# Attention scores: the mask and the row maximum enter the scores through a turned operand, high and low part in one contraction

## The chip, the cores and the metric

The kernel runs on one core of one Trainium2 chip. The metric is the device time of the whole program in microseconds; lower is better. Three timed runs of the kernel before gave 849.24, 849.87 and 851.15 us, median 849.87 us. The trace is of one further, profiled execution.

## The reference

A gated cross-attention layer and a mixture of experts, both with a residual. There are 128 sequences of 64 tokens, width 128, 16 heads of 8 channels, and a context of 64 tokens for each sequence. What matters here is the attention:

```
q, k, v = heads(layernorm(x) @ Wq.T + bq), heads(ctx @ Wk.T + bk), heads(ctx @ Wv.T + bv)
scores  = q k^T / sqrt(8)
scores  = where(pad_mask[key] == 0, -1e9, scores) + src_mask[query, key]
x       = x + tanh(g_xattn) * (softmax(scores) v @ Wo.T + bo)
```

Then `x + tanh(g_ffn) * ffn(layernorm(x))` follows, where ffn takes the two best of 8 experts for each token, a shared expert, and a layer norm. The padding mask depends on the sequence and the key, the source mask on the query and the key.

## The kernel before, in words

Three stages follow one another: `attention` (to about 450 us), `experts` and `combine`. Only the first is touched.

In `attention` a tile is 128 tokens, that is two sequences, b = 0 and 1, on the partitions (64 queries each). There are 64 tiles, and four of them make a quad. Each engine has its own program, written out by hand: a step n handles one tile, and u = n mod 4 is its place in the quad. Work that belongs to a quad (projections of the next quad, its layer norm, its mask, the routing of an earlier one) is put at fixed places u of the steps. Engines meet by semaphores (`need` waits for one). Every engine works strictly in its own order.

TensorE's step n is, in this order: the prefix sums of the routing (u = 1), `project_out(n - 3)`, `scores(n)`, `feed_a` (transposes or a projection for the quad, none at u = 0), `values(n - 2)`, `turn(n - 1)` (eight transposes of the probabilities, L394), `feed_b` (more of the quad's work, L450, L456, L462 or L469), `subtract(n)`.

- `scores` writes 128 x 1024 scores (16 heads of 64 keys) into two PSUM banks in 64x64 tiles of the array (L366). Then it adds the mask with four matmuls of 512 columns (L372): an identity is multiplied with the mask of the queries, spread over 8 heads, once with the high part and once with the low part of the mask, for either half of the heads. The parts are there because the matmuls read the type fp32r, which holds fewer bits than float32.
- `maxima` on VectorE (L531) takes the negated maximum of every query and head. `max_high` and `max_low` (L536, L540) split it into two parts.
- `subtract` (L383) adds the maxima in the same manner: four matmuls of 512 columns, identity times the high or low part, spread over the 64 keys.
- ScalarE takes the exponential from PSUM (L856), the transposes go to PSUM and ScalarE copies them back (L895), `values` forms the sums and the products with v (L403, L410), VectorE divides (L546, L551), and `project_out` multiplies with Wo (L418).

VectorE's step has eight numbered places between its parts. The mask of the next quad is made at u = 2 in four steps (L710, L714, L717, L719), at places 2, 4, 5 and 7; place 2 is before `maxima`, place 4 between `max_high` and `max_low`, place 5 before the reciprocal, place 7 at the end. At u = 3, place 1 adds a bias to a quad of x (L726) and place 2 runs eight aggregations (L585, L586), both before `maxima`. Maxima of tile n need `masked` (the last of the mask's matmuls).

SyncE loads for each quad the context, the padding mask spread to queries by two transfers (`pad_q`, L318) and the padding mask spread to all partitions (`pad_k`, L319).

ScalarE's step has the exponential of tile n - 1 first, then the quad's copies, then the two copies of the turned probabilities.

Of the kernel before, what the change touches and what calls it, by code (L numbers as in the profile page):

```python
# [26 lines left out]
P = 128  # L27
# [28 lines left out]
C_SEL = C_PART + 1  # L56
C_TOKEN = C_SEL + 2

# [26 lines left out]
def constants(NT):  # L85
    c = np.zeros((P, C_TOKEN + NT + steps_listed(NT)), np.float32)
    p = np.arange(P)
    c[:, C_ID:C_ID + P] = np.eye(P)
    c[:, C_TRI:C_TRI + P] = p[:, None] < p[None, :]
    c[:, C_JM:C_JM + HG] = (p[:, None] % 32) // DK == np.arange(HG)[None, :]  # L90
    c[:, C_REV:C_REV + QT * E] = np.tile(E - np.arange(E), QT)
    c[:, C_BASE:C_BASE + E] = np.arange(E) * (NT * P + SL)
    c[:, C_PART] = p
    c[:, C_SEL:C_SEL + 2] = ((p[:, None] // 32) % 2 == np.arange(2)[None, :]) * float(DK) ** -0.5
    c[:, C_TOKEN:C_TOKEN + NT] = NT * P + p[:, None] + P * np.arange(NT)[None, :]
    c[:, C_TOKEN + NT:] = np.arange(steps_listed(NT))
    return c
# [73 lines left out]
def attention(nc, a, NT, lists, m):  # L171
# [6 lines left out]
    with ExitStack() as ctx:  # L178
# [5 lines left out]
        ones_bf = sb("ones_bf", [P, P], BF16)  # L184
        ident_r = sb("ident_r", [P, P])
        w_att = sb("w_att", [P, 4, D])
# [7 lines left out]
        rb = router[:, 32:33]  # L194
        srcm = sb("srcm", [P, S])
        cT = sb("cT", [P, 2, QW])
        pad_q = sb("pad_q", [P, 2, QT, S], I32)
        pad_k = sb("pad_k", [P, 2, QW], I32)
        keep = sb("keep", [P, QW])
        mask = sb("mask", [P, QT, S])  # L200
        mask_hl = sb("mask_hl", [P, 2, 2, QT, S])
        xn = sb("xn", [P, QW])
# [7 lines left out]
        mx = sb("mx", [P, 2, H])  # L210
        mx_hl = sb("mx_hl", [P, 2, 2, H])
        head_ones = sb("head_ones", [P, VS])
# [44 lines left out]
        keep_ready, mask_step, mask_ready, xb_ready = sem("keep_ready"), sem("mask_step"), sem("mask_ready"), sem("xb_ready")  # L257
        masked, maxed, max_split, subbed, exped = (sem(n) for n in ("masked", "maxed", "max_split", "subbed", "exped"))
        turned, PT_ready, att_done, recips, aT_ready = (sem(n) for n in ("turned", "PT_ready", "att_done", "recips", "aT_ready"))
        wo_done, x2_ready = sem("wo_done"), sem("x2_ready")  # L260
# [14 lines left out]
        def exists(item, total):  # L275
            return 0 <= item < total

        LOADS = 4
        CONSTS = 16 * 7
        MASK_STEPS = 4  # L280

# [4 lines left out]

        def wide_mask(part, par, u):

            return mask_hl[:, part, par, u, :].bitcast(F32R).unsqueeze(1).broadcast_to([P, H // 2, S])

# [4 lines left out]
        def _(sp):  # L295
            sp.dma_start(cst[:, :], a["consts"]).then_inc(const_in, 16)
            for t, n in ((w_att, "w_att"), (srcm, "src_mask"), (router, "router"), (cols[:, 0:3], "b_att")):
                sp.dma_start(t if n == "b_att" else t[:], a[n]).then_inc(const_in, 16)
# [9 lines left out]
            def load(q, par):  # L308

                need(sp, v_done, q - 2, total=NQ)  # L310
                need(sp, mask_step, q - 2, per=MASK_STEPS, total=NQ)
                need(sp, kT_ready, q - 2, total=NQ)
                done = quad_in[par]
                sp.dma_start(cT[:, par, :], a["ctx_T"][:, bass.ds(q * QW, QW)]).then_inc(done, 16)
                pads = pad_mask[bass.ds(q * 2 * QT, 2 * QT), :]
                for b in range(2):
                    src = pads.rearrange("(t b) k -> b t k", b=2)[b:b + 1].broadcast_to([S, QT, S])
                    sp.dma_start(pad_q[b * S:(b + 1) * S, par], src).then_inc(done, 16)  # L318
                sp.dma_start(pad_k[:, par].rearrange("p (b k) -> p b k", k=S),  # L319
                             pads.unsqueeze(0).broadcast_to([P, 2 * QT, S])).then_inc(done, 16)  # L320
# [25 lines left out]
        def _(pe):  # L346
# [7 lines left out]
            def scores(n, u, par, q):  # L354
# [118 lines left out]
            def step(j):  # L473
                for v in range(2 * QT):
# [29 lines left out]
        def _(ve):  # L504
# [20 lines left out]
            ve.reciprocal(gates[:, 2:3], gates[:, 2:3]).then_inc(setup_dve, 1)  # L525
            ve.tensor_copy(ident_r[:, :].bitcast(F32R), ident).then_inc(setup_dve, 1)

# [6 lines left out]
            def max_high(n, u):  # L534
                need(ve, maxed, n)
                ve.tensor_copy(mx_hl[:, 0, u % 2, :].bitcast(F32R), mx[:, u % 2, :]).then_inc(max_split, 1)  # L536

            def max_low(n, u):
                need(ve, max_split, n, per=2, k=1)
                ve.tensor_tensor(mx_hl[:, 1, u % 2, :].bitcast(F32R), mx[:, u % 2, :], mx_hl[:, 0, u % 2, :],  # L540
                                 ALU.subtract).then_inc(max_split, 1)

# [161 lines left out]
            def masks(i, j, par, q):  # L704

                p2 = 1 - par
                if i == 0:
                    quad_loaded(ve, j, par, 1)
                    need(ve, mask_step, q, per=MASK_STEPS, total=NQ)
                    ins = ve.tensor_scalar(mask[:, :, :], pad_q[:, p2], 0, NEG, ALU.is_equal, ALU.mult)  # L710
                else:
                    need(ve, mask_step, q + 1, per=MASK_STEPS, k=i, total=NQ)
                if i == 1:
                    ins = ve.tensor_tensor(mask[:, :, :], mask[:, :, :], srcm[:, :].unsqueeze(1).broadcast_to([P, QT, S]),  # L714
                                           ALU.add)
                elif i == 2:
                    ins = ve.tensor_copy(mask_hl[:, 0, p2].bitcast(F32R), mask[:, :, :])  # L717
                elif i == 3:
                    ins = ve.tensor_tensor(mask_hl[:, 1, p2].bitcast(F32R), mask[:, :, :], mask_hl[:, 0, p2],  # L719
                                           ALU.subtract)  # L720
                ins.then_inc(mask_step, 1)
# [28 lines left out]
            def between(place, j, u, par, q):  # L750
# [22 lines left out]
                elif u == 2:  # L773
                    if exists(q + 3, NQ):
# [4 lines left out]
                        elif place == 7:  # L779
                            in_stats(j, par, q, 3, (3,))  # L780
                    if place in (2, 4, 5, 7) and exists(q + 1, NQ):
                        masks((2, 4, 5, 7).index(place), j, par, q)
                else:
# [41 lines left out]
        def _(ac):  # L825
# [22 lines left out]
            def step(j):  # L848
                for v in range(2 * QT):
# [646 lines left out]
def build_inputs(inputs):  # L1496
# [4 lines left out]
    f32["mask_BxS2_ik0"] = g["mask_BxS2_ik0"]  # L1501
    f32["src_mask"] = np.concatenate([g["mask_1x1xSxS2_ff0"][0, 0]] * 2)
    f32["w_att"] = np.stack([g["L0_xattn_" + n].T for n in ("Wq", "Wk", "Wv", "Wo")], axis=1)
# [33 lines left out]
```

## Time and profile before

| what | value |
|---|---|
| timed runs | 849.24, 849.87, 851.15 us |
| profiled execution, its time | 852.03 us |
| its span, first to last instruction | 850.0 us |
| mean granted TensorE clock | 0.941 |
| PE busy | 726.5 us, 85% |
| PE weight loads busy | 591.4 us, 70% |
| VectorE busy | 612.2 us, 72% |
| ScalarE busy | 508.1 us, 60% |
| GpSimd busy | 285.0 us, 34% |

PE is TensorE's matmuls and PEld its weight loads, which may run beside matmuls. Busy times are those of instruction records. Matmuls overlap in the array, so the sum of their durations is more than the time they take one after another. The granted clock is a share of full speed, and 1.00 and 0.50 are TensorE's two levels of 2.4 and 1.2 GHz.

### The profile page before, as it was taken

What the parts mean: (1) busy time and instruction counts of PE and PEld (TensorE: products, weight loads), DVE (VectorE), ACT (ScalarE), POOL (GpSimd) and SP (SyncE); (2) the same over time, 40 slices, a digit from 0 to 9 for tenths busy, and PEclk for the clock granted to TensorE, in tenths of its full rate; (3) what the DMA queues carried; (4) which work ended last, traced back from release to release, by engine and by line L of the source; (5) the groups of instructions that cost most, each with busy time, mean ns of one, the idle gap of its engine ahead of it and who ended that gap; (6) DMA issues with size and microseconds to landing.
All of it is one profiled execution on the core that took longest, in us unless ns stands there. A gap on an engine that the chain in (4) does not pass through costs nothing. (4 is left out here: it accounts for less than half of the span.)

```text
span 850.0 us, 25318 instructions
## 1 busy us (share of the span) xinstructions
PE 726.5 (85%) x8266; PEld 591.4 (70%) x8267; DVE 612.2 (72%) x2341; ACT 508.1 (60%) x1051; POOL 285.0 (34%) x293
## 2 busy tenths in 40 slices
PE   2899999999999999999961029999999999969870
PEld 1577777777777777777740019899999999956650
DVE  5477778778887888877772648766666666627998
ACT  2667777777677776767431006566666666628983
POOL 2000022233332233322257404565555555630000
PEclk9999999999999999999985559999999999989995
DMA  5122212233312233210011662222222222234553
GB/s 128 44 46 46 57 48 59 65 80 82 80 49 62 61 83 83 74 46 33 22 61 63 207 121 58 72 75 75 75 75 77 75 75 72 78 108 128 152 150 96
DMA packets 84289, 66.60 MB, mean 78 GB/s; under 512 B 17008, under 2 KB 71536, under 8 KB 84208
## 3 DMA queue, kind: packets, MB, share of 16 engines
q1 hardware_dynamic: 63008, 35.49, 17.5%
q0 software_dynamic: 8448, 17.45, 6.2%
q10 hardware_dynamic: 12752, 12.58, 4.6%
q8 instruction: 51, 0.84, 0.4%
q14 instruction: 30, 0.25, 0.1%
HBM read 38.21 MB, written 23.09 MB: 72 GB/s over the span
## 5 line engine op out<-in xcount | busy, mean ns | idle before, releaser
L167 POOL DMA_INDIRECT expert_lists<-xn,slots x128 | 128.5, 1004 | 337.8 <-PE pair L410 305.8
L1129 ACT ACTIVATE hT<-pair,b1g_c,gate_c 128x256 f32<-128x256 f32 x272 | 138.3, 562 | 93.6 <-PE pair L76 83.0
L1276 POOL DMA_INDIRECT expert_results<-y,dest x136 | 144.5, 1062 | 130.0 <-DVE y L1245 109.0
L1089 PE MATMUL pair<-w,hT 128*128 x1088 | 134.5, 277 | 0.1
L1089 PEld LDWEIGHTS pair<-w,hT 128*128 128x128 f32 x1088 | 127.0, 192 | 2.7 <-issue 2.0
L531 DVE TENSOR_REDUCE mx<-pair 128x16 f32<-128x1024 f32 x64 | 78.4, 1225 | 46.6 <-PE pair L372 46.6
L856 ACT ACTIVATE prob<-pair 128x1024 f32<-128x1024 f32 x64 | 65.5, 1024 | 45.8 <-PE pair L383 45.7
L895 ACT ACTIVATE PT<-pair 128x512 f32<-128x512 f32 x128 | 69.3, 593 | 38.5 <-PE pair L394 38.5
L74 PE MATMUL pair<-rT,w_now 128*128 128x256 f32 x276 | 84.5, 306 | 2.4 <-DVE rT L68 2.4
L76 PE MATMUL pair<-rT,w_now 128*128 128x256 f32 x276 | 78.9, 286 | 0.0
L75 PE MATMUL pair<-rT,w_now 128*128 128x256 f32 x276 | 78.6, 285 | 0.0
L1216 DVE CAST w_now<-w 128x1024 fp32r x71 | 50.4, 711 | 38.2 <-issue 37.0
L383 PE MATMUL pair<-mx_hl,ident_r 128*128 128x512 f32 x256 | 75.8, 419 | 1.3 <-DVE mx_hl L540 1.3
L372 PE MATMUL pair<-mask_hl,ident_r 128*128 128x512 f32 x256 | 76.9, 422 | 0.0
L366 PE MATMUL pair<-kbd,qg 64*64 64x256 f32 x1024 | 71.0, 393 | 0.0
L394 PE MATMUL pair<-cst,prob 128*128 128x128 f32 x512 | 69.9, 280 | 0.0
L1067 PE MATMUL pair<-cst,rows 128*128 128x128 f32 x140 | 27.3, 277 | 44.3 <-DMA rows<-expert_lists 44.3
L372 PEld LDWEIGHTS pair<-mask_hl,ident_r 128*128 128x128 f32 x256 | 43.4, 189 | 30.6 <-issue 25.0
L546 DVE RECIPROCAL rsum<-pair 128x128 f32<-128x128 f32 x64 | 60.7, 948 | 0.7 <-PE pair L410 0.7
L394 PEld LDWEIGHTS pair<-cst,prob 128*128 128x128 f32 x512 | 54.9, 141 | 5.8
L74 PEld LDWEIGHTS pair<-rT,w_now 128*128 128x128 f32 x276 | 53.4, 193 | 4.1 <-issue 3.7
L66 DVE CAST rT<-pair 128x256 fp32r<-128x256 f32 x70 | 29.6, 424 | 36.4 <-PE pair L1067 36.3
(171 smaller groups left out, 1438.3 us busy)
## 6 DMA issues: line engine op xcount, KB each, us to landing
rows<-expert_lists SPq DMA_DIRECT2D x70, 130.0 KB, 2.2
yin<-expert_results SPq DMA_DIRECT2D x16, 512.0 KB, 5.3
x_all<-in_x SPq DMA_DIRECT2D x16, 256.0 KB, 5.0
cT<-in_ctx_T SPq DMA_DIRECT2D x16, 256.0 KB, 2.9
pad_k<-in_mask_BxS_ik SPq DMA_DIRECT2D x16, 256.0 KB, 4.9
xn2T<-x2T ACTq DMA_DIRECT2D x16, 256.0 KB, 2.4
out<-res ACTq DMA_DIRECT2D x7, 512.0 KB, 4.7
expert_results<-y,dest POOLq DMA_INDIRECT x136
```

The source lines that it names most:

```text
L74: pe.matmul(out, ah, bh, start=True, stop=False)
L75: pe.matmul(out, ah, bl, start=False, stop=False)
L76: return pe.matmul(out, al, bh, start=False, stop=True)
L167: po.indirect_dma_start(lists[:, :], bass.IndirectOffsetOnAxis(ap=m.slots[:, par, t, k:k + 1], axis=0), m.xn2[:, par, t, :], None).then_in ...
L366: pe.matmul(ps[S * b:S * b + S, at:at + 256], qg[rows, par, s, u * P + S * b:u * P + S * b + S], kbd[rows, par, 2 * u + b].rearrange("p j ...
L372: i = pe.matmul(ps[:, half * 512:(half + 1) * 512].rearrange("p (h k) -> p h k", k=S), ident_r[:, :].bitcast(F32R), wide_mask(part, par, u ...
L383: i = pe.matmul(ps[:, half * 512:(half + 1) * 512].rearrange("p (h k) -> p h k", k=S), ident_r[:, :].bitcast(F32R), top.unsqueeze(2).broad ...
L394: t = pe.transpose(pt_ps[h][:, i * P:(i + 1) * P], prob[:, u % 2, p * P:(p + 1) * P], ident)
L531: ve.tensor_reduce(mx[:, u % 2, :], sc_ps[u % 2][:, :].rearrange("p (h k) -> p h k", k=S), X, ALU.max, negate=True).then_inc(maxed, 1)
L1089: last = pe.matmul(y_ps[par][:, h * D:(h + 1) * D], hT[:, par, c, h * P:(h + 1) * P], w2[:, bass.ds(e, 1), c, :].rearrange("p a d -> p (a ...
L1129: ac.activation(hT[:, par, c, :], h_ps[par][c // 2][:, (c % 2) * SL:(c % 2 + 1) * SL], ACT.Gelu, bias=b1g_c[:, c, bass.ds(e, 1)], scale=ga ...
L1276: po.indirect_dma_start(results[:, :], bass.IndirectOffsetOnAxis(ap=dest[:, par, h, :], axis=0), y[:, par, h, :], None).then_inc(sent[par] ...
```

## The change

The roles of the operands in the mask's and the maximum's matmuls are exchanged.

- Mask: the mask is now kept with the key on the partition and the query in the free dimension. The high part stands on partitions 0 to 63 and the low part on 64 to 127. It is the stationary operand, and a constant selector of keys (`key_r`, 1 where the partition modulo 64 is the key) is the moving one, so a contraction over 128 partitions adds both parts. Two matmuls instead of four for a tile.
- Maximum: `max_high` and `max_low` write the parts into a 128 x 128 tile, two copies at columns 0 to 31 and 64 to 95. TensorE turns 96 columns of it with one transpose (`turn_maxima`, into the scores buffer of the other tile), ScalarE copies that to `mT`, and `subtract` contracts 32 rows (16 heads, high and low) with a constant selector of heads (`head_r`). The first half of the heads uses rows 0 to 31, the second rows 64 to 95. Two matmuls instead of four for a tile.
- The mask of a quad is made from a constant source mask, turned on the host, and padding columns that are computed once, so `pad_q` and its two transfers for each quad are gone, and there is one more constant to load. The mask's steps are three instead of four, and place 4 is empty.

```diff
-                    for part in range(2):
-                        i = pe.matmul(ps[:, half * 512:(half + 1) * 512].rearrange("p (h k) -> p h k", k=S),
-                                      ident_r[:, :].bitcast(F32R), wide_mask(part, par, u),
-                                      start=False, stop=False, skip_group_check=True)
+                    i = pe.matmul(ps[:, half * 512:(half + 1) * 512].rearrange("p (h k) -> p h k", k=S),
+                                  mask_hl[:, par, 2 * u:2 * u + 2, :].rearrange("p b q -> p (b q)").bitcast(F32R),
+                                  key_r[:, :].bitcast(F32R).unsqueeze(1).broadcast_to([P, H // 2, S]),
+                                  start=False, stop=False, skip_group_check=True)
                 i.then_inc(masked, 1)
 
+            def turn_maxima(n, u):
+                need(pe, max_split, n, per=2)
+                need(pe, exped, n - 1)
+                pe.transpose(sc_ps[(u + 1) % 2][0:S + 2 * H, 0:P], mx_hl[:, u % 2, 0:S + 2 * H], ident)\
+                  .then_inc(max_turned, 1)
+
             def subtract(n, u):
-                need(pe, max_split, n, per=2)
+                need(pe, max_flat, n)
                 ps = sc_ps[u % 2]
                 for half in range(2):
-                    for part in range(2):
-                        top = mx_hl[:, part, u % 2, half * 8:half * 8 + 8].bitcast(F32R)
-                        i = pe.matmul(ps[:, half * 512:(half + 1) * 512].rearrange("p (h k) -> p h k", k=S),
-                                      ident_r[:, :].bitcast(F32R), top.unsqueeze(2).broadcast_to([P, H // 2, S]),
-                                      start=False, stop=(part == 1), skip_group_check=True)
+                    rows = slice(S * half, S * half + 2 * H)
+                    i = pe.matmul(ps[:, half * 512:(half + 1) * 512].rearrange("p (h k) -> p h k", k=S),
+                                  mT[rows, u % 2, :].bitcast(F32R),
+                                  head_r[rows, half * 8:half * 8 + 8].bitcast(F32R).unsqueeze(2)
+                                  .broadcast_to([2 * H, H // 2, S]),
+                                  start=False, stop=True, skip_group_check=True)
                 i.then_inc(subbed, 1)
...
                         values(n - 2, (u - 2) % QT, par if u >= 2 else 1 - par)
+                    if exists(n, NT):
+                        turn_maxima(n, u)
                     if exists(n - 1, NT):
                         turn(n - 1, (u - 1) % QT)
...
             ve.tensor_copy(key_r[:, :].bitcast(F32R), cst[:, C_KEY:C_KEY + S]).then_inc(setup_dve, 1)
+            ve.tensor_copy(head_r[:, :].bitcast(F32R), cst[:, C_HEAD:C_HEAD + H]).then_inc(setup_dve, 1)
+            ve.tensor_scalar(pad_neg[:, :], pad_T[:, :], 0, NEG, ALU.is_equal, ALU.mult).then_inc(setup_dve, 1)
+            ve.memset(mx_hl[:, :, :], 0.0).then_inc(setup_dve, 1)
+            ve.wait_ge(setup_dve, 15)
...
-                ve.tensor_copy(mx_hl[:, 0, u % 2, :].bitcast(F32R), mx[:, u % 2, :]).then_inc(max_split, 1)
+                ve.tensor_copy(both_copies(mx_hl, u, 0).bitcast(F32R), mx[:, u % 2, :].unsqueeze(1).broadcast_to([P, 2, H]))\
+                  .then_inc(max_split, 1)
...
-                    ins = ve.tensor_scalar(mask[:, :, :], pad_q[:, p2], 0, NEG, ALU.is_equal, ALU.mult)
+                    pads = pad_neg[:, (q + 1) * 2 * QT:(q + 2) * 2 * QT]
+                    ins = ve.tensor_tensor(mask[:, :, :], srcT[:, :].unsqueeze(1).broadcast_to([P, 2 * QT, S]),
+                                           pads.unsqueeze(2).broadcast_to([P, 2 * QT, S]), ALU.add)
...
                 if i == 1:
+                    ins = ve.tensor_copy(mask_hl[:, p2].bitcast(F32R), mask[:, :, :])
                 elif i == 2:
+                    ins = ve.tensor_tensor(mask_hl[S:, p2].bitcast(F32R), mask[S:, :, :], mask_hl[S:, p2], ALU.subtract)
...
+                    if exists(n, NT):
+                        need(ac, max_turned, n)
+                        need(ac, subbed, n - 2)
+                        ac.activation(mT[0:S + 2 * H, u % 2, :].bitcast(F32R), sc_ps[(u + 1) % 2][0:S + 2 * H, 0:P],
+                                      ACT.Copy).then_inc(max_flat, 1)
```

The last piece stands in ScalarE's step just before the copies of the turned probabilities of tile n - 1.

## Rows read from the trace of the kernel before

**Rows 1.** Busy time in a stretch: us, busy us (count) by engine, clock, DMA share, GB/s.
```profile
200.00:300.00 100.00, 100.00 (x1415) 74.27 (x1414) 80.32 (x334) 71.71 (x134) 32.01 (x32) 1.00 0.27 70
```

**Rows 2.** Waits, 60 to 370 us: waiter, releaser, us in total, times, longest.
```profile
DVE mx L531 <- PE pair L372: 26.2, 48, 0.8
```

**Rows 3.** Timeline of PE, 204 to 230 us: start, us, line, op, count [idle before].
```profile
203.77 0.40 PE L372 MATMUL pair<-mask_hl,ident_r 128*128 128x512 f32 x1
...
205.12 1.09 PE L394 MATMUL pair<-cst,prob 128*128 128x128 f32 x8
...
209.49 1.20 PE L372 MATMUL pair<-mask_hl,ident_r 128*128 128x512 f32 x4
...
212.08 1.09 PE L394 MATMUL pair<-cst,prob 128*128 128x128 f32 x8
...
214.31 0.39 PE L418 MATMUL pair<-w_att,aT 128*128 128x128 f32 x2
214.62 1.09 PE L366 MATMUL pair<-kbd,qg 64*64 64x256 f32 x16
215.65 1.21 PE L372 MATMUL pair<-mask_hl,ident_r 128*128 128x512 f32 x4
...
218.66 1.09 PE L394 MATMUL pair<-cst,prob 128*128 128x128 f32 x8
219.68 0.43 PE L462 MATMUL pair<-x2T,router 128*32 128x128 f32 x8
...
222.34 1.19 PE L372 MATMUL pair<-mask_hl,ident_r 128*128 128x512 f32 x4
...
224.60 1.09 PE L394 MATMUL pair<-cst,prob 128*128 128x128 f32 x8
...
228.63 1.20 PE L372 MATMUL pair<-mask_hl,ident_r 128*128 128x512 f32 x4
```

**Rows 4.** Timeline of VectorE, one tile at u = 0: from maximum to low part.
```profile
204.21 1.23 DVE L531 TENSOR_REDUCE mx<-pair 128x16 f32<-128x1024 f32 x1 [0.58 <-PE pair L372]
...
205.68 0.18 DVE L540 TENSOR_TENSOR mx_hl<-mx,mx_hl 128x16 fp32r<-128x16 f32 x1
```

**Rows 5.** L383 at tile 0, and L372 at 202 us: duration ns min/median/max, starts.
```profile
L383 PE MATMUL pair<-mx_hl,ident_r x4: 379/379/484, 31.5 to 32.3; 128*128 128x512 f32 x4
```
```profile
L372 PE MATMUL pair<-mask_hl,ident_r x4: 393/398/496, 203.0 to 203.8; 128*128 128x512 f32 x4
```

**Rows 6.** Timeline of PE weight loads around tile 0's subtraction.
```profile
31.51 0.73 PEld L383 LDWEIGHTS pair<-mx_hl,ident_r 128*128 128x128 f32 x4 [1.70 <-DVE mx_hl L540]
```

**Rows 7.** Timeline of VectorE: the maxima of the tiles at u = 2 and 3.
```profile
216.89 1.23 DVE L531 TENSOR_REDUCE mx<-pair 128x16 f32<-128x1024 f32 x1 [0.83 <-PE pair L372]
...
223.58 1.22 DVE L531 TENSOR_REDUCE mx<-pair 128x16 f32<-128x1024 f32 x1 [0.32 <-PE pair L372]
```

**Rows 8.** Groups by line, 60 to 370 us: shapes, count, busy us, mean ns, idle before.
```profile
L726 DVE TENSOR_TENSOR x_all<-x_all,bo_row 128x512 f32<-128x512 f32 x12 | 8.1, 674 | 0.0
...
L714 DVE TENSOR_TENSOR mask<-mask,srcm 128x256 f32<-128x256 f32 x12 | 5.0, 419 | 0.0
L719 DVE TENSOR_TENSOR mask_hl<-mask,mask_hl 128x256 fp32r<-128x256 f32 x12 | 4.9, 407 | 0.0
...
L903 ACT ACTIVATE LT<-pair,router 128x128 f32<-128x128 f32 x11 | 4.1, 371 | 0.0
...
L717 DVE CAST mask_hl<-mask 128x256 fp32r<-128x256 f32 x12 | 3.5, 295 | 0.0
L710 DVE TENSOR_SCALAR mask<-pad_q 128x256 f32<-128x256 int32 x12 | 3.3, 276 | 0.0
```

**Rows 9.** Timeline of ScalarE at u = 1, ahead of the copies of probabilities.
```profile
212.05 0.71 ACT L845 ACTIVATE kbd<-kT,cst 128x512 f32<-128x512 f32 x1
```

**Rows 10.** Timeline of the start: a constant's transfer is issued, VectorE's setup.
```profile
3.52 0.43 SPq L300 DMA_DIRECT2D gates<-in_gates  x1
```
```profile
9.13 0.21 DVE L526 CAST ident_r<-cst 128x128 fp32r<-128x128 f32 x1
```

More of the change, by code:

```diff
@@ L56 @@
 C_SEL = C_PART + 1
-C_TOKEN = C_SEL + 2
+C_KEY = C_SEL + 2
+C_HEAD = C_KEY + S
+C_TOKEN = C_HEAD + H
 def split(ve, done, high, low, x):
@@ L94, in constants @@
     c[:, C_SEL:C_SEL + 2] = ((p[:, None] // 32) % 2 == np.arange(2)[None, :]) * float(DK) ** -0.5
+    c[:, C_KEY:C_KEY + S] = p[:, None] % S == np.arange(S)[None, :]
+    c[:, C_HEAD:C_HEAD + H] = (p[:, None] % S < 2 * H) & (p[:, None] % H == np.arange(H)[None, :])
     c[:, C_TOKEN:C_TOKEN + NT] = NT * P + p[:, None] + P * np.arange(NT)[None, :]
@@ L184, in attention @@
         ones_bf = sb("ones_bf", [P, P], BF16)
-        ident_r = sb("ident_r", [P, P])
+        key_r = sb("key_r", [P, S])
+        head_r = sb("head_r", [P, H])
         w_att = sb("w_att", [P, 4, D])
@@ L194, in attention @@
         rb = router[:, 32:33]
-        srcm = sb("srcm", [P, S])
+        srcT = sb("srcT", [P, S])
+        pad_T = sb("pad_T", [P, 2 * NT], I32)
+        pad_neg = sb("pad_neg", [P, 2 * NT])
         cT = sb("cT", [P, 2, QW])
-        pad_q = sb("pad_q", [P, 2, QT, S], I32)
         pad_k = sb("pad_k", [P, 2, QW], I32)
         keep = sb("keep", [P, QW])
-        mask = sb("mask", [P, QT, S])
-        mask_hl = sb("mask_hl", [P, 2, 2, QT, S])
+        mask = sb("mask", [P, 2 * QT, S])
+        mask_hl = sb("mask_hl", [P, 2, 2 * QT, S])
         xn = sb("xn", [P, QW])
@@ L210, in attention @@
         mx = sb("mx", [P, 2, H])
-        mx_hl = sb("mx_hl", [P, 2, 2, H])
+        mx_hl = sb("mx_hl", [P, 2, P])
+        mT = sb("mT", [P, 2, P])
         head_ones = sb("head_ones", [P, VS])
@@ L258, in attention @@
         masked, maxed, max_split, subbed, exped = (sem(n) for n in ("masked", "maxed", "max_split", "subbed", "exped"))
+        max_turned, max_flat = sem("max_turned"), sem("max_flat")
         turned, PT_ready, att_done, recips, aT_ready = (sem(n) for n in ("turned", "PT_ready", "att_done", "recips", "aT_ready"))
@@ L276, in exists @@
             return 0 <= item < total
-        LOADS = 4
-        CONSTS = 16 * 7
-        MASK_STEPS = 4
+        LOADS = 2
+        CONSTS = 16 * 8
+        MASK_STEPS = 3
         J0, J1 = -1, NQ // 2 + 2
@@ L285, in cols_of, with both_copies @@
             return bass.ds(t * D, n * D)
-        def wide_mask(part, par, u):
-            return mask_hl[:, part, par, u, :].bitcast(F32R).unsqueeze(1).broadcast_to([P, H // 2, S])
+        def both_copies(t, u, part):
+            return t[:, u % 2, :].rearrange("p (c w) -> p c w", w=S)[:, :, part * H:part * H + H]
         block = ctx.enter_context(nc.Block())
@@ L296, in _ @@
             sp.dma_start(cst[:, :], a["consts"]).then_inc(const_in, 16)
-            for t, n in ((w_att, "w_att"), (srcm, "src_mask"), (router, "router"), (cols[:, 0:3], "b_att")):
+            for t, n in ((w_att, "w_att"), (srcT, "src_T"), (pad_T, "pad_T"), (router, "router"), (cols[:, 0:3], "b_att")):
                 sp.dma_start(t if n == "b_att" else t[:], a[n]).then_inc(const_in, 16)
@@ L315, in load @@
                 pads = pad_mask[bass.ds(q * 2 * QT, 2 * QT), :]
-                for b in range(2):
-                    src = pads.rearrange("(t b) k -> b t k", b=2)[b:b + 1].broadcast_to([S, QT, S])
-                    sp.dma_start(pad_q[b * S:(b + 1) * S, par], src).then_inc(done, 16)
                 sp.dma_start(pad_k[:, par].rearrange("p (b k) -> p b k", k=S),
@@ L525, in _ @@
             ve.reciprocal(gates[:, 2:3], gates[:, 2:3]).then_inc(setup_dve, 1)
-            ve.tensor_copy(ident_r[:, :].bitcast(F32R), ident).then_inc(setup_dve, 1)
+            ve.tensor_copy(key_r[:, :].bitcast(F32R), cst[:, C_KEY:C_KEY + S]).then_inc(setup_dve, 1)
+            ve.tensor_copy(head_r[:, :].bitcast(F32R), cst[:, C_HEAD:C_HEAD + H]).then_inc(setup_dve, 1)
+            ve.tensor_scalar(pad_neg[:, :], pad_T[:, :], 0, NEG, ALU.is_equal, ALU.mult).then_inc(setup_dve, 1)
+            ve.memset(mx_hl[:, :, :], 0.0).then_inc(setup_dve, 1)
+            ve.wait_ge(setup_dve, 15)
             def maxima(n, u):
@@ L535, in max_high @@
                 need(ve, maxed, n)
-                ve.tensor_copy(mx_hl[:, 0, u % 2, :].bitcast(F32R), mx[:, u % 2, :]).then_inc(max_split, 1)
+                ve.tensor_copy(both_copies(mx_hl, u, 0).bitcast(F32R), mx[:, u % 2, :].unsqueeze(1).broadcast_to([P, 2, H]))\
+                  .then_inc(max_split, 1)
             def max_low(n, u):
                 need(ve, max_split, n, per=2, k=1)
-                ve.tensor_tensor(mx_hl[:, 1, u % 2, :].bitcast(F32R), mx[:, u % 2, :], mx_hl[:, 0, u % 2, :],
-                                 ALU.subtract).then_inc(max_split, 1)
+                ve.tensor_tensor(both_copies(mx_hl, u, 1).bitcast(F32R), mx[:, u % 2, :].unsqueeze(1).broadcast_to([P, 2, H]),
+                                 both_copies(mx_hl, u, 0), ALU.subtract).then_inc(max_split, 1)
             def sums_inverse(n, u):
@@ L713, in masks @@
                 if i == 1:
-                    ins = ve.tensor_tensor(mask[:, :, :], mask[:, :, :], srcm[:, :].unsqueeze(1).broadcast_to([P, QT, S]),
-                                           ALU.add)
+                    ins = ve.tensor_copy(mask_hl[:, p2].bitcast(F32R), mask[:, :, :])
                 elif i == 2:
[L717 to L720, printed above, removed]
+                    ins = ve.tensor_tensor(mask_hl[S:, p2].bitcast(F32R), mask[S:, :, :], mask_hl[S:, p2], ALU.subtract)
                 ins.then_inc(mask_step, 1)
@@ L780, in between @@
                             in_stats(j, par, q, 3, (3,))
-                    if place in (2, 4, 5, 7) and exists(q + 1, NQ):
-                        masks((2, 4, 5, 7).index(place), j, par, q)
+                    if place in (2, 5, 7) and exists(q + 1, NQ):
+                        masks((2, 5, 7).index(place), j, par, q)
                 else:
@@ L1501, in build_inputs @@
     f32["mask_BxS2_ik0"] = g["mask_BxS2_ik0"]
-    f32["src_mask"] = np.concatenate([g["mask_1x1xSxS2_ff0"][0, 0]] * 2)
+    f32["src_T"] = np.concatenate([g["mask_1x1xSxS2_ff0"][0, 0].T] * 2)
+    f32["pad_T"] = np.concatenate([g["mask_BxS2_ik0"].T] * 2)
     f32["w_att"] = np.stack([g["L0_xattn_" + n].T for n in ("Wq", "Wk", "Wv", "Wo")], axis=1)
```

1 line of the change is left out of this document (removed).

## The prediction

> **What bounds the kernel now.** First I read the busy table by stretch, to find the limit of the stage that changes. In a stretch in its middle PE is busy for all 100.00 of 100 us at clock 1.00, against 80.32 us of VectorE and 71.71 us of ScalarE [rows 1]. The reader is to see an engine that never waits. The waits confirm it from the other side: VectorE waits for the mask's last matmul before each maximum, 26.2 us in 48 waits, so about 0.55 us of slack for each tile [rows 2]. So time is made by PE's own order, and I read its timeline tile by tile. A tile's last mask matmul ends at 203.77 + 0.40 = 204.17, the same point of the next quad is 228.63 + 1.20 = 229.83, so a quad lasts 25.66 us; the pattern repeats through the stage. I write every event relative to the end of a tile's mask matmuls, because that starts VectorE's chain. The transposes of the probabilities (L394) start at 0.95, 1.39, 1.80 and 1.07 us for u = 0, 1, 2, 3 [rows 3]. (The mask ends are 204.17, 210.69, 216.86 and 223.53.) The new transpose of the maxima stands just ahead of them, so these four numbers decide the case.
>
> **The mask's matmuls.** Four matmuls take 1.20 us. Without the last one's 0.40 and the first one's extra 0.10 (496 ns against 398, its weights being loaded in sight) they follow one another by (1.20 - 0.10 - 0.40)/3 = 0.23 us [rows 3, 5]. Two fewer save 0.46 us for each tile, 1.86 us for a quad. I take the two that remain at the same pace. A constant moving operand might run at the subtraction's pace of 0.217 (next part) but not slower in any row.
>
> **The subtraction.** Its four matmuls start from 31.5 to 32.3 and the first is 105 ns longer than the others when its weights are loaded after a wait [rows 5]. Weight loads there span 0.73 us for three intervals and a load of 0.19, or (0.73 - 0.11 - 0.19)/2 = 0.217 us for each matmul, one interval being short by the exposed first [rows 6]. The two new ones use different row groups (0 to 31, 64 to 95) and different banks. No row has this shape. Nearest are the scores: 16 records of 256 columns in 1.09 us, where two records of 128 columns in `project_out` start 0.39 - 0.28 = 0.11 apart (eight such in L394 take 1.09, which is seven paces of 0.11, 0.05 for the first load and a duration of about 0.27), so 256 columns alone take 0.22 and 16 in series would take 3.5 us [rows 3]. They run four at a time, two of them row halves into two banks. So the pair should start together, and one interval is left: saved 3 x 0.217 = 0.65 us a tile. The other end is a pair in series, saved 0.43 us. I take the first, by the scores.
>
> **New switches of the array's shape.** The array was in 128x128 shape from the transposes through `subtract` to `project_out`. Now `subtract` is in 32x128 shape. The price of a switch: `project_out`'s second matmul starts at 214.42, its pace would end it at 214.53, and the scores start at 214.62, so 0.09 us is lost; then the first matmul behind a bare 128-column load is 0.10 us longer [rows 3, 5]. That is 0.20 us on entry and 0.20 on exit. At u = 2 L462 has already left the shape, so the entry is free. Four exits and three entries make 1.4 us a quad; prefix sums behind the exit at u = 0 to 1 have cheap loads, so I take 1.32. Bounds: 0.09 for each switch if loads are hidden (0.63 a quad), and 0.20 for each of eight (1.6).
>
> The Trainium skill (TensorEngine Tiling, Key Properties) says "Changing tiling mode (not just tile) drains the TensorE". By that rule alone the seven switches cost the 0.09 that the trace shows as its drain, and the quad would gain 0.7 us more than in my sum; the rows put the exposed load beside it, so I keep 0.20. The trace agrees with the rule (the 0.09 us before the scores).
>
> **The new transpose.** One record of 128 columns at a pace of 0.11 us (1.09 - 0.27 over 7 intervals is 0.117, the first load's 0.05 among it) [rows 3]: +0.44 us a quad. Its load takes the exposed place that the first probability's load had.
>
> **The new wait, the heart of it.** Formerly the split maximum was needed by `subtract`, after the transposes and `feed_b`. Now it is needed before them. VectorE's chain from the mask's end: 0.04 to the reduction, and the low part ends at 205.68 + 0.18 = 205.86, that is 1.69 [rows 4]. Two splits write 32 instead of 16 values each (estimate +0.02 each, from 256 more values costing 0.27 us between L719 and L726 [rows 8]), and PE's load starts about 0.04 after the release: 1.77 us. At u = 2 a mask step stood between the splits and is gone, so 1.77 holds there too. Behind the waiting transpose stand the eight transposes of tile n - 1, `feed_b` and `subtract`, and all else of PE. Stalls without further delay: 0.82, 0.38, 0 and 0.70 us.
>
> Further delay comes because VectorE must be free when the mask ends, which is now 0.46 us earlier behind `project_out`. Its idle before the maximum was 0.58 at u = 0 and 0.83 at u = 2 and 0.32 at u = 3 [rows 4, 7]; I take 0.45 at u = 1 by the mean of rows 2. At u = 3 that is short by 0.14. At u = 2 the first mask step grows from 0.276 to 0.674 (L710 to the shape of L726), so 0.83 - 0.40 - 0.46 leaves -0.03 [rows 7, 8]. Stalls then: 0.82, 0.40, 0 and 0.85, sum 2.07 us.
>
> **VectorE's other work.** The mask was 0.276 + 0.419 + 0.295 + 0.407 = 1.40 us a quad; it becomes 0.674 (add), about 0.43 (cast of 512, by the slope of L717), 0.674 (64 partitions, 512 values): 1.78 [rows 8]. Together +0.38 and +0.16 for the splits, on an engine at 20.6 of 25.65. At 21.1 of 25.0 us it is still not the bound, so this costs nothing beyond the delays counted: the later mask steps lie behind the divide that `project_out` needs. If that cover went, 0.4 us a quad.
>
> **ScalarE's new copy** (96x128 from PSUM, by L903's 0.371 us [rows 8]) runs beside the eight transposes (0.88 us) and `feed_b` (0.4 to 0.9). At u = 1 ScalarE is busy until 212.05 + 0.71 = 212.76, or 2.07 after the mask's end [rows 9]; the turned maxima are there at about 1.8 + 0.33 = 2.1, so no delay arises. The copies of probabilities come 0.37 later and are used a step later. Cost nothing; if the cover went, 0.4 us a tile.
>
> **Loads.** `pad_q` goes, off the path. In the start one more constant is issued before the one that VectorE waits for (+0.47, an issue of 0.43 and its gap), and setup exchanges one cast of 0.21 for two casts, a scalar operation, a memset and a wait (smaller tiles than the cast's; estimate 0.15 each, less 0.2: +0.4) [rows 10]. VectorE's chain sets the start, so +0.9 us.
>
> **Sum.** A quad: stalls +2.07, mask -1.86, subtraction -2.60, transpose +0.44, switches +1.32: -0.63 us. Fourteen full quads: -8.8. The last quad has no `feed` work before the transposes, so all four tiles wait as at u = 0, 0.82 (3.3 together): +0.6. In the first, early tiles waited for VectorE already and the detour over ScalarE takes the place of the two saved matmuls: about +0.5. Start +0.9. Total -6.8 us: 852.03 - 6.8 = 845.2 for a profiled execution. That one lies 2.2 above the median of the runs, so the timed median should be 849.87 - 6.8 = **843.1 us**.
>
> **Rivals.**
> 1. *The pair of `subtract` runs in series* (slower). Place: L383's successors, 0.217 us more for each of 64 tiles, +13.9: 849.87 - 6.8 + 13.9 = 857.0. It decides as soon as more than half of the overlap is missing. For it: no row has 32x128 tiles, and two wide fp32r streams go at once. Against it: the scores' four at a time.
> 2. *The wait eats the gain.* The maximum's chain is later than 1.77 us, by 0.15 us at three tiles (VectorE not free, a slower split with two copies), or the switches cost 0.05 more each: +0.4 to 0.6 a quad, 849 to 850. For it: VectorE has only the slack above, and it grows. Against: stalls at u = 2 are nearly zero, which leaves that tile its full saving.
> 3. *Switches cost only their drain*, the loads being pulled ahead: -0.7 a quad more, 832 us. For it: weight loads run beside matmuls elsewhere. Against: the 105 and 100 ns in rows 5.
> 4. *The change doesn't do what it says*, the wide matmuls being no limit: excluded by the first reading, PE without idle.
>
> **Chances.** My forecast 0.60 (own range 838 to 848), rival 1 0.17, rival 2 0.14, rival 3 0.09. A change within 0.2% (1.7 us) is about what a measurement can't tell from none. Faster: 0.60 + 0.09 less a little = 0.68. Same: most of rival 2, 0.13. Slower: rival 1 and the rest, 0.19. The range 835 to 854 leaves out most of rival 1 and the end of rival 3. The forecast's number, 843.1.
>
> **What would show it.** Right: PE's timeline gets idle time or late loads before the new transpose, released by VectorE's low part, of about 0.8, 0.4, 0 and 0.85 us; the two L383 successors start within 0.01 us; gaps of 0.20 at both ends of them; the quad's period is 25.0. Wrong: the pair 0.217 apart; waits for ScalarE's copy in front of `subtract`; a period above 25.65.

## The result, and the profile after

Four timed runs of the changed kernel took 839.2 to 841.7 us, median 840.33, beside 850.47 for the kernel before. The ratio is 0.9873, with a 95% interval of 0.9856 to 0.9890: 1.3% faster. The forecast was 6.8 us less; 10.1 us by the medians and 10.8 by the ratio were measured, and the profiled span fell from 850.0 to 837.6. Here and below, executions more than 1.5% above the fastest of the same kernel are left out of medians and ratios (one of e1's ten, five of e5's ten, one of e7's six).

The first view is again the busy table by stretch. Its row answers rows 1.

```profile
200.00:300.00 100.00, 93.66 (x1444) 63.30 (x1445) 85.20 (x344) 78.09 (x155) 31.23 (x32) 1.00 0.23 67
```

PE is no longer busy all the time: it stands for 6.3 us of 100. The waits (rows 2 before) name the reason. VectorE's long wait for the mask's matmuls, 26.2 us before, is nearly gone (1.5 us). TensorE now waits for VectorE instead: 26 such waits stand in the some 50 tiles of that stretch, 17.7 us in all.

```profile
PE pair L385 <- DVE mx_hl L559: 17.7, 26, 1.1
...
PE pair L448 <- DVE kT L715: 2.2, 11, 0.2
DVE mx L549 <- PE pair L376: 1.5, 4, 0.4
```

PE's timeline of one quad answers rows 3 (L376 is the mask, L385 the new transpose, L406 the probabilities' transposes, L393 the subtraction):

```profile
199.67 0.73 PE L376 MATMUL pair<-key_r,mask_hl 128*128 128x512 f32 x2
...
202.16 0.31 PE L385 MATMUL pair<-cst,mx_hl 128*96 128x128 f32 x1 [0.74 <-DVE mx_hl L559]
202.31 1.04 PE L406 MATMUL pair<-cst,prob 128*128 128x128 f32 x8
...
206.26 0.73 PE L376 MATMUL pair<-key_r,mask_hl 128*128 128x512 f32 x2
207.20 0.63 PE L448 MATMUL pair<-cst,xn 128*128 128x128 f32 x4 [0.20 <-DVE kT L715]
...
208.81 0.31 PE L385 MATMUL pair<-cst,mx_hl 128*96 128x128 f32 x1
...
210.37 0.48 PE L393 MATMUL pair<-head_r,mT 32*128 32x512 f32 x2
210.78 0.49 PE L430 MATMUL pair<-w_att,aT 128*128 128x128 f32 x2
...
212.22 0.73 PE L376 MATMUL pair<-key_r,mask_hl 128*128 128x512 f32 x2
...
214.77 0.32 PE L385 MATMUL pair<-cst,mx_hl 128*96 128x128 f32 x1
...
218.10 0.74 PE L376 MATMUL pair<-key_r,mask_hl 128*128 128x512 f32 x2
...
220.61 0.31 PE L385 MATMUL pair<-cst,mx_hl 128*96 128x128 f32 x1 [0.65 <-DVE mx_hl L559]
...
224.47 0.73 PE L376 MATMUL pair<-key_r,mask_hl 128*128 128x512 f32 x2
```

A quad now takes 224.47 - 199.67 = 24.80 us, 0.86 less than [rows 3]. Counted from the end of each tile's mask matmuls, the new transpose starts at 1.76, 1.82, 1.82 and 1.77 us for u = 0 to 3, where L394 stood at 0.95, 1.39, 1.80 and 1.07. Two matmuls in 0.48 us, each of 478 ns, start together.

VectorE's timeline of the same tile (rows 4), the maximum at u = 3 (rows 7), and the setup (rows 10):

```profile
200.44 1.22 DVE L549 TENSOR_REDUCE mx<-pair 128x16 f32<-128x1024 f32 x1
...
201.92 0.19 DVE L559 TENSOR_TENSOR mx_hl<-mx,mx_hl 128x32 fp32r<-128x32 f32 x1
```
```profile
218.85 0.15 DVE L605 BATCH_NORM_AGGREGATE mv<-st 128x2 f32<-128x6 f32 x1
218.92 1.19 DVE L549 TENSOR_REDUCE mx<-pair 128x16 f32<-128x1024 f32 x1
```
```profile
7.20 0.23 DVE L520 CAST tri_bf<-cst 128x128 bf16<-128x128 f32 x1 [7.09 <-DMA gates<-in_gates]
```

The low part is ready 1.71 us after the mask's end (202.11 - 200.40). At u = 3 the maximum has no idle time before it any more: VectorE comes from its aggregations 0.05 us late.

### The profile page after: what moved, and what is told of

It is laid out like the page before. It is cut to its first block and busy times, and to the rows that moved or that the text cites. A ratio compares the mean times of both kernels' runs of the same rounds, so it can differ in the third digit from the quotient of the medians.

```text
span 837.6 us, 25065 instructions
## 1 busy us (share of the span) xinstructions
PE 686.2 (82%) x8074; PEld 537.2 (64%) x8075; DVE 621.1 (74%) x2328; ACT 523.3 (62%) x1115; POOL 280.5 (33%) x293
## 5 line engine op out<-in xcount | busy, mean ns | idle before, releaser
L171 POOL DMA_INDIRECT expert_lists<-xn,slots x128 | 124.3, 971 | 330.4 <-PE pair L422 297.9
L549 DVE TENSOR_REDUCE mx<-pair 128x16 f32<-128x1024 f32 x64 | 77.9, 1217 | 14.1 <-PE pair L376 12.6
L406 PE MATMUL pair<-cst,prob 128*128 128x128 f32 x512 | 66.4, 273 | 0.0
L576 DVE SCALAR_TENSOR_TENSOR x_all<-pair,gates,x_all 128x128 f32<-128x128 f32 x64 | 22.4, 351 | 53.6 <-PE pair L430 52.7
L406 PEld LDWEIGHTS pair<-cst,prob 128*128 128x128 f32 x512 | 56.6, 141 | 0.1
L76 PEld LDWEIGHTS pair<-rT,w_now 128*128 128x128 f32 x276 | 53.3, 193 | 3.3 <-issue 2.1
L77 PEld LDWEIGHTS pair<-rT,w_now 128*128 128x128 f32 x276 | 53.5, 194 | 0.0
L78 PEld LDWEIGHTS pair<-rT,w_now 128*128 128x128 f32 x276 | 53.3, 193 | 0.0
```

What stands on the lines that cost most here:

```text
L76: pe.matmul(out, ah, bh, start=True, stop=False)
L77: pe.matmul(out, ah, bl, start=False, stop=False)
L78: return pe.matmul(out, al, bh, start=False, stop=True)
L171: po.indirect_dma_start(lists[:, :], bass.IndirectOffsetOnAxis(ap=m.slots[:, par, t, k:k + 1], axis=0), m.xn2[:, par, t, :], None).then_in ...
L406: t = pe.transpose(pt_ps[h][:, i * P:(i + 1) * P], prob[:, u % 2, p * P:(p + 1) * P], ident)
L549: ve.tensor_reduce(mx[:, u % 2, :], sc_ps[u % 2][:, :].rearrange("p (h k) -> p h k", k=S), X, ALU.max, negate=True).then_inc(maxed, 1)
```

## The experiments

All ratios are to the kernel before on the same chip. Several chips were used. The code shown is one piece of each edit. On the chip of e1 to e4 the kernel before takes 852 us, about as for the result. Quads are means over tiles 16 to 51 of each trace.

| run | us | before | ratio, 95% interval | quad, us |
|---|---|---|---|---|
| changed kernel | 840.3 | 850.5 | 0.987 (0.986 to 0.989) | 24.81 |
| e1, pair in series | 855.2 | 852.2 | 1.005 (1.003 to 1.007) | 25.65 |
| e2, mask alone | 827.7 | 852.2 | 0.972 (0.969 to 0.975) | 24.25 |
| e3, maximum alone | 869.1 | 852.2 | 1.021 (1.017 to 1.024) | 26.80 |
| e4, transpose between | 826.1 | 852.2 | 0.970 (0.967 to 0.973) | 23.99 |
| e5, no switch | 893.0 | 892.3 | 1.000 (0.996 to 1.004) | 26.99 |
| e6, mask alone, keys early | 864.0 | 892.3 | 0.971 (0.966 to 0.975) | 24.68 |
| e7, between, keys early | 876.5 | 892.3 | 0.981 (0.978 to 0.985) | 25.02 |
| e8, behind, keys early | 869.4 | 892.3 | 0.974 (0.970 to 0.978) | 24.60 |
| e9, e8 again | 872.4 | 891.6 | 0.976 (0.970 to 0.982) | 24.59 |
| e10, e6 again | 863.0 | 891.6 | 0.965 (0.959 to 0.971) | 24.70 |
| e11, changed kernel again | 870.9 | 869.9 | 1.002 (1.000 to 1.004) | 26.30 |
| e12, e8 a third time | 845.8 | 869.9 | 0.973 (0.970 to 0.977) | 24.33 |

**e1: the pair of the subtraction in series**

```diff
-                    rows = slice(S * half, S * half + 2 * H)
+                    rows = slice(0, 2 * H)
```

> The changed kernel, with both matmuls of the subtraction on rows 0 to 31, so that they can't run side by side. Theory (the pair runs side by side and PE's order sets the time): the second one starts 0.217 us after the first, 64 x 0.217 = 13.9 us more than the changed kernel's 840.3, so 854. Rival (the two only start together, and the longer records and the late project_out show that the banks or the streams take turns): no more than 3 us more, 840 to 843.

```profile
203.13 0.69 PE L393 MATMUL pair<-head_r,mT 32*128 32x512 f32 x2
203.76 0.49 PE L430 MATMUL pair<-w_att,aT 128*128 128x128 f32 x2
```

The pair takes 0.69 instead of 0.48 us, the quad 0.84 us more (4 x 0.21), and the time is 855.2 for an expected 854. So the two row groups do run side by side, and the pair in series would have made the change a loss. The theory holds; rival 1 of the prediction falls.

**e2 and e3: each half by itself**

```diff
# e2: the changed kernel with the old subtraction
-                    if exists(n, NT):
-                        turn_maxima(n, u)
# e3: the kernel before with the new subtraction
+                    if exists(n, NT):
+                        turn_maxima(n, u)
```

> The mask's half of the change alone: two matmuls with the turned mask, the new mask steps, no pad_q, but the old subtraction with four matmuls and an identity. Theory (the mask's half brings the whole gain, 0.466 us a tile, and the maximum's half costs more than it brings): a quad of 25.65 - 1.86 = 23.8 us, 850.5 - 30 + 1 for the start = 821. Rival 1 (both halves bring something): 843 to 848. Rival 2 (VectorE, with 21.0 us of work a quad, becomes the bound): quad not below 24.4, 830.

> The maximum's half alone: transpose of the split maxima, ScalarE's copy, two matmuls of 32 rows; the mask as before with four matmuls, four steps and pad_q. Theory: stalls before the new transpose of 0.81, 0.42, 0.13 and 0.70 us, less 0.94 for the subtraction net of switches and transpose, is +1.1 us a quad, +17, 867. Rival (two matmuls fewer are a gain, the stall hides in other slack): 840 to 850.

The maximum's half alone costs 16.8 us, as expected (17): a quad of 26.80, 1.15 more. The mask's half alone brings 24.6 us, more than the whole change, but 5 less than expected (850.5 - 821 = 29.5). Its trace shows where they went (L374 is the mask there, L439 the transposes of `xn`):

```profile
223.19 0.74 PE L374 MATMUL pair<-key_r,mask_hl 128*128 128x512 f32 x2
224.12 0.63 PE L439 MATMUL pair<-cst,xn 128*128 128x128 f32 x4 [0.20 <-DVE kT L702]
```

At u = 1 PE goes on from the mask to transposes that write the bank out of which VectorE makes the keys (L702), a step before its maximum. The four mask matmuls used to cover it. Now PE stands: the start of the last matmul of `values` moves from 1.24 to 1.63 us after the mask's end, and 0.39 us in each of 15 quads is 5.9 us. So it is the order of one step, and not VectorE's sum of work (rival 2), that PE waits for there; e6 below moves that step. In the changed kernel the same wait lies inside the wait for the maximum, which is why the halves don't add up: -1.40 and +1.15 us a quad make -0.25, and -0.85 was measured. By tiles, 0.44 of these 0.60 lie at u = 1, where both halves pay for about the same wait, and 0.17 at u = 2, where in e3 the mask's step between the splits delays the maximum by 0.15. In e2 the tiles at u = 0, 2 and 3 are shorter by 0.46 to 0.47, which is what the matmuls give, so nothing is left for the loads of `pad_q` that went.

**e4: the transpose of the maxima between the halves of the others**

```diff
-                    if exists(n, NT):
-                        turn_maxima(n, u)
                     if exists(n - 1, NT):
-                        turn(n - 1, (u - 1) % QT)
+                        turn(n - 1, (u - 1) % QT, (0,))
+                    if exists(n, NT):
+                        turn_maxima(n, u)
+                    if exists(n - 1, NT):
+                        turn(n - 1, (u - 1) % QT, (1,))
```

> The changed kernel, with the transpose of the maxima moved from ahead of the eight transposes of the probabilities to between the first four and the last four. Theory (the wait for VectorE's split is what is left to win): stalls of 0.81 and 0.72 us at u = 0 and 3 shrink by about 0.49 each, so 1.0 us a quad less, 825. Rival (the copy on ScalarE then comes too late for the subtraction, or the copies of the probabilities too late for values): no gain, 838 to 845, with waits for L911 or for the copies in the trace.

```profile
209.64 0.66 PE L406 MATMUL pair<-cst,prob 128*128 128x128 f32 x4
210.13 0.27 PE L385 MATMUL pair<-cst,mx_hl 128*96 128x128 f32 x1
210.24 0.60 PE L406 MATMUL pair<-cst,prob 128*128 128x128 f32 x4
...
212.98 0.73 PE L376 MATMUL pair<-key_r,mask_hl 128*128 128x512 f32 x2
...
214.78 0.66 PE L406 MATMUL pair<-cst,prob 128*128 128x128 f32 x4
215.50 0.31 PE L385 MATMUL pair<-cst,mx_hl 128*96 128x128 f32 x1
```

The first three lines are u = 2, where nothing was left to win, the last three u = 3. There the transpose of the maxima still starts 1.79 us after the mask's end (213.71), but four other transposes are already done. The tiles at u = 0 and 3 are each 0.43 us shorter than in the changed kernel (6.16 and 5.95 against 6.59 and 6.38), and the time is 826.1 for an expected 825. So the wait for the split was most of what was left to win, and the copy on ScalarE stays hidden. This kernel beats both the kernel before (3.0%) and the changed one (by about 15 us, 0.970 against 0.987 of the kernel before), with the whole change in it. Against the mask's half alone (e2) it is only 1.6 us less, 0.2%, with overlapping intervals: even well placed, the maximum's half earns next to nothing.

**e5: no switch of shape**

```diff
-                    rows = slice(S * half, S * half + 2 * H)
+                    rows = slice(0, P)
```

with `head_r` zero outside rows 0 to 31, and 128 columns turned and copied.

> The changed kernel, with the subtraction as two matmuls over all 128 rows instead of 32: the whole 128x128 tile is turned and copied, and the head selector is zero except on rows 0 to 31. The pair no longer runs side by side, but the array keeps its 128x128 shape from the transposes to project_out. Theory (the shape switches around the subtraction cost 0.19 us on entry at u = 0, 1, 3, 0.19 on exit at u = 1, 2, 3 and 0.09 at u = 0): 1.24 us less and 4 x 0.217 = 0.87 us more a quad, -0.37, so about 6 us under the changed kernel's 840.3: 834. Rival (those gaps come from the operand that ScalarE has just written or from the transpose, not from the shape): they stay, +14 us, 854.

It ran on another chip, where the kernel before takes 892 us and unexplained gaps arise at u = 3 and delay u = 0 (below), and its ten executions range from 885 to 905 us. So its time, 893.0, says nothing on 6 us. Its trace, of an execution of 905.1 us, does where no gap is:

```profile
226.86 0.70 PE L393 MATMUL pair<-head_r,mT 128*128 128x512 f32 x2
227.39 0.38 PE L430 MATMUL pair<-w_att,aT 128*128 128x128 f32 x2
```

From the new transpose to the next scores, tiles at u = 1 and 2 take 2.271 and 2.337 us against 2.393 and 2.304 in the changed kernel. One serial interval costs 0.217; so two switches were worth 0.34 at u = 1 and the one at u = 2, where L474 (L462 before) has left the shape anyway, 0.18. The exit's first matmul starts 0.21 after the last of the pair (227.39 against 226.86 + 0.32) and not 0.41. So the gaps come with the shape, as the theory says, at 0.17 to 0.18 us each for an expected 0.19. The total is not measured.

**e6, e7, e8: the keys' step earlier, and the transpose last**

```diff
                         kept_keys(j, par, q)
+                        keys(q + 1)
                 elif u == 1:
...
-                    if place == 2 and exists(q + 1, NQ):
-                        keys(q + 1)
```

This is the edit that the three share. e6 has it on e2, e7 on e4, and e8 has the transpose of the maxima behind all eight others beside it.

> The mask's half alone, and VectorE's step that makes the keys of the next quad (it frees the PSUM bank that the transposes at u = 1 write) moved from u = 1, place 2, just before the maximum, to the end of u = 0. Theory (the mask's half missed its 30 us because at u = 1 PE, 0.46 us earlier at those transposes, now waits 0.39 us for that step): the wait goes, quad 24.25 - 0.39 = 23.86, 827.7 - 6 = 821.5. Rival (VectorE's sum of work is the bound, 87% busy, and the delay only moves): 826 to 828.

> The changed kernel with the transpose of the maxima between the two halves of the others, and the keys' step moved to the end of u = 0 as in the run beside it. Theory: at u = 1 the transpose of the maxima starts at 1.88 after the mask's end instead of 2.27, so 0.39 us a quad less than the 826.05 of the kernel without the move: 820. Rival (VectorE's sum of work is the bound): 825 to 827.

> As the run beside it, but the transpose of the maxima stands behind all eight others. Theory: the last stalls for VectorE's split, 0.32 and 0.23 us at u = 0 and 3, go too; at u = 1 and 2 the copy on ScalarE, 0.68 us from the transpose to the weights' load, may show by 0.0 to 0.2 us: 0.2 to 0.5 us a quad less, 812 to 817. Rival (the copy is now exposed at all four tiles): 820 or more, with waits for L911's successor in the trace.

None of the three times came near: 864, 876 and 869. The local part holds. In e6 and e7 the last matmul of `values` at u = 1 starts at 1.24 after the mask again (the tile takes 5.81 us in e6 against 6.14 in e2), and e7's transpose starts at 1.88 as expected. But in all three the maximum at u = 3 starts 1.0 to 1.4 us after the mask's end, from the fourth quad on, where e4 has 0.09, and VectorE has nothing to do in between. The kernel before took 892 us there, so either the chip or the order made it. On this one chip the mask's half alone (e6) is again no slower than the whole change with the transpose last (e8).

**e9 to e12: chip or order?** e9 and e12 are e8, e10 is e6, and e11 is the changed kernel, all unaltered.

> The kernel with the transpose of the maxima behind all eight others and the keys' step early, once more: its first run was on another chip, on which the kernel before took 892 us and VectorE stood for 1.35 us before the maximum at u = 3 with no work and no releaser. Theory (those gaps belong to that chip): without them 24.60 - 1.26 (u = 3) - 0.28 (u = 0) = 23.1 us a quad, and 840.3 - 16 x 1.7 = 813. Rival (the gaps come with this order of the work): a quad of 24.6, about 838.

> The mask's half alone with the keys' step early, once more, for the same reason. Theory (PE's wait for the keys' step at u = 1 was what the mask's half missed, and the gaps at u = 3 belong to the other chip): a quad of 23.86 and 821.5. Rival (VectorE's sum of work is the bound): 826 to 828.

> The changed kernel itself, unaltered. If it falls on a chip on which the kernel before takes about 892 us: theory (the gaps of 1.35 us before the maximum at u = 3 belong to those chips, whatever the order of the work) a quad of 26.1 instead of 24.8, and the gaps in its trace at the same place; rival (the gaps come with the changed order of the last experiments) 24.8 and no gap. If it falls on a chip with 850 to 852 us: 840.

> The kernel with the transpose of the maxima behind all eight others and the keys' step early, beside it. On a chip with 850 to 852 us for the kernel before: 813 by the theory that its gaps belong to the other chips, 838 by the rival. On a chip with 892 us: 870 as before, and the difference to the changed kernel beside it is what the order brings there (theory: 20 us or more, as 1.4 us a quad by the stalls taken away).

Both repeats fell on a third chip of the slow kind (891.6) and showed the same gaps, on average to 0.03 us, so they could not tell. e11 does: the changed kernel itself, on a fourth chip, has the gap. VectorE's timeline, with the mask's end at 227.21, and PE's of the same moment:

```profile
226.48 0.73 PE L376 MATMUL pair<-key_r,mask_hl 128*128 128x512 f32 x2
...
227.71 0.27 PE L422 MATMUL pair<-PT,vb 128*32 128x64 f32 x2
228.44 0.70 PE L422 MATMUL pair<-PT,vb 128*32 128x64 f32 x30 [0.46 <-issue]
```
```profile
227.24 0.15 DVE L605 BATCH_NORM_AGGREGATE mv<-st 128x2 f32<-128x6 f32 x1
228.59 1.23 DVE L549 TENSOR_REDUCE mx<-pair 128x16 f32<-128x1024 f32 x1 [1.20 <-PE pair L376]
```

The row names PE as releaser only because that event came last; PE had been done for 1.38 us (228.59 - 227.21), and it stops in the middle of a group of matmuls itself. The quad is 26.30 for an expected 26.1 (named for a chip of 892 us), and the kernel is that of the result, whose trace has no such gap: the gap belongs to the chip. On that chip the change brings nothing (1.002, interval 1.000 to 1.004).

e12 beside it takes 845.8, 25 us less than the changed kernel for an expected "20 or more". A quad is 1.97 us shorter, so the later transpose and the earlier keys' step together are worth the expected 1.4 us there and more; what each of the two brings was not separated. The 813 us expected on a chip of the first kind was not measured.

## Why the prediction was right, step by step

The sign, the place and the mechanism held: 843.1 forecast, 840.3 measured, in the range. That it came so near is in part luck, as the steps and their sum below show. By steps of the prediction, for a quad of the chip of the result (means of 36 tiles):

- **Mask's matmuls**: forecast -1.86. The last scores matmul to the mask's end fell from 1.504 to 1.038 us, four times 0.466: -1.86. Exact.
- **The subtraction, the switches, the transpose**: forecast -2.60 + 1.32 + 0.44 = -0.84. From L394 or L385 to the next scores, u = 0 to 3 fell by 0.27, 0.15, 0.36 and 0.16: -0.94. The pair starts 3 ns apart. Most of the 0.1 us of difference is the price of a switch, 0.19 and not 0.20 at six places, and the exit at u = 0, about 0.09 and not 0.12, behind which the prefix sums' light weights load.
- **The new wait**: forecast stalls 0.82, 0.40, 0, 0.85, sum 2.07. Measured 0.81, 0.43, 0, 0.72, sum 1.95. The chain of 1.77 us held to 0.01 at u = 0. At u = 1 the number came out for a reason that I had not seen. There PE loses its time first, at the wait for the keys' step (L448, [0.20 <-DVE kT L715] above): in e4, which has nothing for the maximum to hold up at that point, the transposes of the probabilities start at 1.78, 0.39 later than before. Only the 0.04 from 1.78 to 1.82 is left for the maximum. Either wait alone would have cost about 0.4; that they coincide was luck. At u = 3 I had VectorE 0.15 us late; it was 0.05 late. VectorE's steps overlap when nothing is waited for: the maximum starts at 218.92, before the last aggregation ends (218.85 + 0.15), so its idle time of 0.32 was worth 0.08 more than I gave it.
- **Sum of a quad**: -0.85 instead of -0.63. Over the 14 full quads the trace has -11.6 us (tile 4 to tile 60) where I had -8.8.
- **The last quad**: forecast +0.6, measured -1.0, a failed step. The new waits came much as forecast (2.9 us in four, for 3.3), but I took the kernel before as bound by PE alone there, and it had waits of its own. PE stood for the division at u = 1 and for ScalarE's normalisation, and after the change for neither. These are 1.03 of the 1.6 us; the rest was not traced:

```profile
413.82 0.19 PE L422 MATMUL pair<-oh_bf,tri_bf 128*128 128x32 bf16 x1 [0.47 <-DVE aT L551]
...
419.33 0.66 PE L456 MATMUL pair<-cst,xn 128*128 128x128 f32 x4 [0.56 <-ACT xn L875]
```

- **The start**: forecast +0.9 for loads and setup and +0.5 for the first quad. VectorE's setup begins 0.63 us later (7.20 against 6.57), the first mask ends 0.57 later, tile 4 ends 0.53 later. VectorE reaches its first statistics 1.21 us later (10.46 against 9.25), so the longer setup was real, but only 0.57 of it reaches the first mask: that VectorE's chain alone sets the start was a wrong step. The first quad's own loss did not come.
- **The sum**: the three misses, 2.8, 1.6 and 0.9 us, all go the same way, so by the trace the attention stage became 12.1 us shorter for a forecast 6.8. The two traced executions lie 12.6 us apart (852.03 and 839.41), the medians only 10.1, and that spread brought the measured time back towards my number.
- **ScalarE's copy**: forecast 0.37 us and hidden. It takes 0.27 and is hidden but for two waits of 0.6 us in all between 60 and 370 us; e8 shows the price when it isn't: at u = 2 the subtraction follows the transpose by 0.64 us, which is that copy with its two hand-overs.

What I did not ask is what each half is worth by itself, though my own sum held the answer: mask -1.86, all the rest +1.23. e2 and e3 confirm it, but for the wait that e2 uncovered. The whole change brings 10 us where its better half alone brings 24.6. Rival 2 (the wait eats the gain) is what the maximum's half does by itself; rival 3 (switches at the price of the drain, 0.09) falls by e5, with 0.17 to 0.18 us a switch.

And the forecast was tied to one kind of chip. What it left out is the slack that the change uses up. Before, the low part of the maximum was ready at 1.68 us and needed by L383 at 2.80 at u = 3, 1.1 us of cover. The change spends that cover. A maximum that starts 1.3 us late then goes into the path whole: the tile at u = 3 is 7.71 us in e11 against 6.38, +1.33. With the old subtraction (e10 against e2) the same tile is 6.58 against 5.82, +0.76, of which PE's own gap is 0.37. That the kernel before loses less than the changed one on such chips is thus argued from e10 and from the times (870.9 and 869.9 side by side); the kernel before was not traced there. Of the 32 us by which e11's span exceeds the result's, 20 lie before the last tile's mask (436.6 us against 417.0).

## What to carry to other kernels

Price each half of a change alone: "half as many wide matmuls" was 1.86 us a quad where the operands only changed roles, and a loss where it needed a detour over VectorE, TensorE and ScalarE in the middle of an in-order program. When a result is needed earlier than before, look at what stands behind the waiting instruction and put that ahead of it; moving one transpose behind four others was worth about 15 us. And slack that a change uses up may also be its protection against disturbances that the profiled chip does not show.

## What the runs showed of the hardware

- Two matmuls of 32 rows and 512 columns in different row groups and banks start 3 ns apart and take 478 ns each, against 379 for a 128-row one behind others; on the same rows the second starts 0.32 after the first, 0.10 of it the bare load.
- A change of the array's shape to or from the 32-row pair costs 0.09 us without a start and 0.10 us more on the next matmul of float32 weights. At u = 1 of the result's trace the pair starts 0.09 us after the pace of L468 allows, and L430's first record is 377 ns instead of 275. Measured against e5, which has no change there, each is worth 0.17 to 0.18. With the prefix sums' weights (bf16) next, it is about 0.09.
- At least four chips, three levels for the same kernel before: 850 to 852, 870 and 892 us (two chips). On the slower three, from the quad on in which GpSimd's scatters begin, VectorE stands for 0.8 to 1.25 us before the maximum at u = 3 of every quad (and in e8 and e9 for up to 0.36 at u = 0), and TensorE's `values` end 0.4 us (e6, e10) or 0.7 to 0.8 us (the others) late at the same moment, each with nothing to wait for in the profile. The mask's end there lies beside the third scatter of a batch, which ends 0.46 us after it, and 2.4 to 2.9 us behind the issue of `xn2T`'s transfer. But both stand at the same place in the traces of the result and of e4, without a gap. Neither a cause nor the reason for the other time lost on those chips was found.
